# A four-layer graph network: more node-stage work on GpSimd, a bias by TensorE, and sums zeroed by ScalarE

## The reference, cut to what matters

```python
h = maximum(layernorm(x), 0); x = x + gat(h)      # layer 0, 8 heads of 16, self loops
h = maximum(layernorm(x), 0); x = x + gcn(h)      # layer 1
h = maximum(layernorm(x), 0); x = x + pna(h)      # layer 2
h = maximum(layernorm(x), 0); x = x + gatv2(h)    # layer 3
```

## Time and profile before

| | before |
|---|---|
| median of three runs | 4756.52 us (4754.43 to 4757.53) |
| profiled execution, its own time | 4756.6 us |
| span of that execution | 4754.8 us |
| mean granted TensorE clock | 0.729 |
| PE busy | 3336.3 us (70%) |
| PEld busy | 2878.0 us (61%) |
| DVE busy | 3192.4 us (67%) |
| ACT busy | 2417.6 us (51%) |
| POOL busy | 3323.1 us (70%) |

### The profile page before, as it was taken

One profiled execution on the slowest core, in us unless ns is written; L12 is line 12 of the kernel. 1 busy time (PEld: TensorE's weight loads), 2 busy tenths in 40 slices (PEclk: granted clock), 3 DMA queues, 4 the chain that ended last, 5 costly groups with the idle time before them and its releaser, 6 DMA issues. The chain is left out here.

```text
span 4754.8 us, 95466 instructions
## 1 busy us (share of the span) xinstructions
PE 3336.3 (70%) x21401; PEld 2878.0 (61%) x21402; DVE 3192.4 (67%) x8183; ACT 2417.6 (51%) x5426; POOL 3323.1 (70%) x3505
## 2 busy tenths in 40 slices
PE   3888888887533333334577777777696888888886
PEld 2666666666533333333476676767564777777775
DVE  5888888888533333334677777787656676666767
ACT  3666666665300000000577777777535666666664
POOL 4777777775677777776677777777524777777774
PEclk7555555555755566655799999899897888888887
DMA  7333333332122121111366666666422333333332
GB/s 131 88 84 86 86 84 86 86 86 54 49 52 53 53 53 53 53 53 44 120 184 184 185 185 185 181 186 183 145 63 50 76 79 80 80 80 80 79 78 72
DMA packets 367220, 462.19 MB, mean 97 GB/s; under 512 B 104067, under 2 KB 271235, under 8 KB 367104
## 3 DMA queue, kind: packets, MB, share of 16 engines
q0 software_dynamic: 107648, 226.35, 20.4%
q1 hardware_dynamic: 254176, 233.02, 16.3%
q10 hardware_dynamic: 5280, 1.58, 0.1%
HBM read 327.40 MB, written 134.06 MB: 97 GB/s over the span
## 5 line engine op out<-in xcount | busy, mean ns | idle before, releaser
L856 POOL DMA_INDIRECT e_G<-dr_tab,src_idx x832 | 810.3, 974 | 266.6 <-issue 253.2
L856 POOL DMA_INDIRECT m_G<-dr_tab,src_idx x832 | 798.2, 959 | 262.7 <-issue 246.4
L856 POOL DMA_INDIRECT v_G<-dr_tab,src_idx x832 | 791.5, 951 | 264.5 <-issue 248.3
L1749 POOL DMA_INDIRECT s_G<-dr_tab,chunk_src x784 | 740.0, 944 | 241.9 <-issue 238.6
L1837 PE MATMUL s_OUT<-s_G,s_S 128*128 x1664 | 380.2, 421 | 586.1 <-SPq L1781 578.4
L1837 PEld LDWEIGHTS s_OUT<-s_G,s_S 128*128 128x128 f32 x1664 | 354.7, 324 | 611.4 <-issue 611.4
L1793 DVE TENSOR_TENSOR ACC<-ACC,s_OUT 128x129 f32 x832 | 241.3, 290 | 604.5 <-PE s_OUT L1837 500.8
L1261 PE MATMUL e_OUT<-e_RH,e_S 128*128 128x144 f32 x1664 | 512.4, 476 | 2.4 <-DVE e_RH L1147 2.4
L2277 ACT COPY f_AT<-r_TP 128x512 f32<-128x512 f32 (+1 forms) x13 | 7.2, 555 | 973.6 <-PE r_TP L2299 973.6
L1994 DVE TENSOR_TENSOR ACC<-ACC,m_OUT 128x256 f32 x832 | 347.3, 417 | 222.3 <-PE m_OUT L2077 126.2
L1261 PEld LDWEIGHTS e_OUT<-e_RH,e_S 128*128 128x128 f32 x1664 | 405.3, 327 | 35.8 <-DVE e_RH L1147 18.4
(11 more groups left out here) (380 smaller groups left out, 8123.9 us busy)
## 6 DMA issues: line engine op xcount, KB each, us to landing
dr_ends<-m_XB SPq DMA_DIRECT2D x416, 256.0 KB, 3.2
e_LR<-dr_row_loc SPq DMA_DIRECT2D x104, 256.0 KB
m_MS<-dr_row_start SPq DMA_DIRECT2D x104, 256.0 KB
v_LR<-dr_row_loc SPq DMA_DIRECT2D x104, 256.0 KB
e_G<-dr_tab,src_idx POOLq DMA_INDIRECT x832
m_G<-dr_tab,src_idx POOLq DMA_INDIRECT x832
v_G<-dr_tab,src_idx POOLq DMA_INDIRECT x832
s_G<-dr_tab,chunk_src POOLq DMA_INDIRECT x784, 2.5
```

What stands on the lines that cost most here:

```text
L856: pool.indirect_dma_start(out=out, out_offset=None, in_=table, in_offset=bass.IndirectOffsetOnAxis(ap=g["src_idx"][:, step:step + 1], axis ...
L1749: pool.indirect_dma_start(out=G[:, c % (RING * GROUP), 0:D], out_offset=None, in_=table[:, :], in_offset=bass.IndirectOffsetOnAxis(ap=g["c ...
```

## The change

What it does, place by place:

- `gat_pass` and `moments_pass`: `ACC` is zeroed by an ACT instruction (a copy with scale 0 of a broadcast column) ahead of ACT's other work there, not by DVE's memset. `sum_pass` keeps its memset.
- `gat_pass`, behind the gathers: POOL computes the own loop's logit and 0.2 times it, in place in `XPA`; `gat_to_gcn` has two DVE instructions fewer.
- `gat_to_gcn`: POOL weighs the own rows (`by_head` with `es`), 13 pieces, and scales the table rows of the pieces 1, 3, 6, 8 and 11 (`on_pool`), behind its `add_rows` of the same piece. PE waits for both semaphores. SP waits, piece by piece, for the engine that scaled it.
- `pna_to_gatv2`: POOL normalises (`normalise_rows`: multiply and add with two scalars per row, without the rectifier), one piece behind its `row_root`; ACT rectifies when it copies the turned piece. PE adds the own rows' bias with one more product per tile (a row of ones by `b3`), and ACT copies them out negated, in place of DVE.
- The last block: DVE does pieces 0 to 6 as before. For pieces 7 to 12 ACT scales per tile, POOL adds the bias, ACT rectifies and POOL adds onto `X`. SP stores the pieces of both as they come.

The diff, cut to its core:

```diff
+        self.on_pool = [j for j in range(self.n) if j % 5 in (1, 3)]
...
+    def normalise_rows(self, pool, j):
+
+        pool.wait_ge(self.nmr_done, j + 1)
+        wait(pool, self.turned, j - self.R + 1)
+        for u in range(self.width(j)):
+            t = j * self.ch + u
+            ins = pool.tensor_scalar(self.H[:, j % self.R, u, :], self.g["X"][:, t, :], self.rstd[:, t:t + 1], self.nmr[:, t:t + 1],
+                                     ALU.mult, ALU.add)
+        ins.then_inc(self.h_done, 1)
...
+    def row_taken(self, j):
+
+        here = [i for i in range(j + 1) if (i in self.on_pool) == (j in self.on_pool)]
+        return (self.pool_taken if j in self.on_pool else self.taken), len(here)
...
-            out = self.HT[:, j % 2, 0:self.width(j), :]
-        self.nc.scalar.copy(out, self.TP[:, j % 2, 0:self.width(j) * P].rearrange("p (u n) -> p u n", n=P)).then_inc(self.ht_in, 1)
+            out, func = self.HT[:, j % 2, 0:self.width(j), :], ACT.Relu
+        self.nc.scalar.activation(out, self.TP[:, j % 2, 0:self.width(j) * P].rearrange("p (u n) -> p u n", n=P), func).then_inc(self.ht_in, 1)
...
+                pool.tensor_tensor(own_slope, own_slope, destination, ALU.add).then_inc(own_logits, 1)
+                pool.wait_ge(own_logits, 1)
+                pool.tensor_scalar(destination, own_slope, SLOPE, 0.0, ALU.mult, ALU.add).then_inc(own_logits, 1)
+                pool.wait_ge(own_logits, 2)
...
+                nc.scalar.activation(ACC[:].rearrange("p t c -> p (t c)"), g["ones"][:, 0:1].to_broadcast([P, TILES * AC]), ACT.Copy,
+                                     scale=0.0).then_inc(acc_done, 1)
...
-                V.memset(ACC[:], 0.0).then_inc(acc_done, 1)
...
+                nc.scalar.activation(ACC[:].rearrange("p t c -> p (t c)"), g["ones"][:, 0:1].to_broadcast([P, TILES * 2 * D]), ACT.Copy,
+                                     scale=0.0).then_inc(acc_done, 1)
...
-                V.memset(ACC[:], 0.0).then_inc(acc_done, 1)
...
+        def scale_rows(eng, j, done):
+            eng.tensor_tensor(T[:, st.tiles(j), :], st.H[:, j % st.R, 0:st.width(j), :],
+                              g["rs_out"][:, st.tiles(j)].unsqueeze(2).to_broadcast([P, st.width(j), D]), ALU.mult).then_inc(done, 1)
...
+                pool.wait_ge(chain, CHAIN)
+                for j in range(st.n):
+                    by_head(pool, XPA, es, j, own_scaled)
                 st.column_root(pool)
+                pool.wait_ge(rs_root, 1)
                 for j in range(st.n + 2):
                     if j < st.n:
                         st.row_root(pool, j)
                     if j >= 2:
                         st.add_rows(pool, j - 2)
+                        if j - 2 in st.on_pool:
+                            scale_rows(pool, j - 2, st.pool_taken)
...
-                    sp.wait_ge(st.taken, j + 1)
+                    sp.wait_ge(*st.row_taken(j))
...
+                    pe.wait_ge(rows_scaled, j + 1)
                     pe.wait_ge(own_scaled, j + 1)
...
-                c.then(V.tensor_tensor(es[:], XPA[:, :, D:D + HEADS], XPA[:, :, D + HEADS:], ALU.add))
-                c.then(V.tensor_scalar(mx[:], es[:], SLOPE, None, ALU.mult))
-                c.then(V.tensor_tensor(es[:], es[:], mx[:], ALU.max))
-                c.then(V.tensor_tensor(mx[:], r[:], es[:], ALU.max))
+                c.then(V.tensor_tensor(es, es, XPA[:, :, D + HEADS:], ALU.max))
...
-                        by_head(ACC, r, j, rows_scaled)
-                        by_head(XPA, es, j, own_scaled)
+                        by_head(V, ACC, r, j, rows_scaled)
...
-                    if i >= 0:
+                    if i >= 0 and i not in st.on_pool:
                         dve.wait_ge(st.h_done, i + 1)
-                        V.tensor_tensor(T[:, st.tiles(i), :], st.H[:, i % st.R, 0:st.width(i), :],
-                                        g["rs_out"][:, st.tiles(i)].unsqueeze(2).to_broadcast([P, st.width(i), D]),
-                                        ALU.mult).then_inc(st.taken, 1)
+                        scale_rows(V, i, st.taken)
...
-                for j in range(st.n):
-                    st.row_root(pool, j)
+                for j in range(st.n + 1):
+                    if j < st.n:
+                        st.row_root(pool, j)
+                    if j >= 1:
+                        st.normalise_rows(pool, j - 1)
...
-                for j in range(st.n + 3):
+                for j in range(st.n + 4):
                     if j < st.n:
                         st.apply(act, j)
-                    if 0 <= j - 2 < st.n:
-                        st.normalise(act, j - 2)
-                    if j >= 3:
+                    if 0 <= j - 3 < st.n:
                         st.turned_in(act, j - 3)
+                    i = j - 4
+                    if i >= 0:
+                        act.wait_ge(st.product, i + 1)
+                        nc.scalar.activation(XR[:, st.tiles(i), :], OP[:, 2 * (i % 2) + 1, 0:st.width(i) * D].rearrange("p (u d) -> p u d", d=D),
+                                             ACT.Copy, scale=-1.0).then_inc(xr_in, 1)
...
+                        wait(pe, xr_in, i - 1)
                         for u in range(st.width(i)):
                             nc.tensor.matmul(OP[:, 2 * (i % 2), u * (D + 1):(u + 1) * (D + 1)], st.HT[:, i % 2, u, :],
                                              g["W3"][:, 0:D + 1], start=True, stop=True)
-                            ins = nc.tensor.matmul(OP[:, 2 * (i % 2) + 1, u * D:(u + 1) * D], st.HT[:, i % 2, u, :],
-                                                   g["W3"][:, D + 1:2 * D + 1], start=True, stop=True)
+                            own = OP[:, 2 * (i % 2) + 1, u * D:(u + 1) * D]
+                            nc.tensor.matmul(own, g["ones"][0:1, :], g["b3"][0:1, D + 1:2 * D + 1], start=True, stop=False)
+                            ins = nc.tensor.matmul(own, st.HT[:, i % 2, u, :], g["W3"][:, D + 1:2 * D + 1], start=False, stop=True)
...
-                                        per_feature(g["b3"][:, 0:D + 1], w), ALU.add)
-                        V.scalar_tensor_tensor(XR[:, st.tiles(i), :], OP[:, 2 * (i % 2) + 1, 0:w * D].rearrange("p (u d) -> p u d", d=D), -1.0,
-                                               per_feature(g["b3"][:, D + 1:2 * D + 1], w), ALU.mult, ALU.subtract).then_inc(st.taken, 1)
+                                        per_feature(g["b3"][:, 0:D + 1], w), ALU.add).then_inc(st.taken, 1)
...
-                for j in range(NCH):
+                for j in range(HERE):
...
+            @block.scalar
+            def _(act):
+                def rectify(j):
+                    tl = slice(j * CH, min((j + 1) * CH, TILES))
+                    act.wait_ge(biased, j - HERE + 1)
+                    nc.scalar.activation(ACC[:, tl, 1:D + 1], ACC[:, tl, 1:D + 1], ACT.Relu).then_inc(rectified, 1)
+
+                act.wait_ge(denominators, 2)
+                for j in range(HERE, NCH):
+                    for t in range(j * CH, min((j + 1) * CH, TILES)):
+                        ins = nc.scalar.activation(ACC[:, t, 1:D + 1], ACC[:, t, 1:D + 1], ACT.Copy, scale=rd[:, t:t + 1])
+                    ins.then_inc(scaled, 1)
+                    if j > HERE:
+                        rectify(j - 1)
+                rectify(NCH - 1)
+
+            @block.gpsimd
+            def _(pool):
+                def add(j):
+                    tl = slice(j * CH, min((j + 1) * CH, TILES))
+                    pool.wait_ge(rectified, j - HERE + 1)
+                    pool.tensor_tensor(g["X"][:, tl, :], g["X"][:, tl, :], ACC[:, tl, 1:D + 1], ALU.add).then_inc(other_rows, 1)
+
+                for j in range(HERE, NCH):
+                    tl = slice(j * CH, min((j + 1) * CH, TILES))
+                    pool.wait_ge(scaled, j - HERE + 1)
+                    pool.tensor_tensor(ACC[:, tl, 1:D + 1], ACC[:, tl, 1:D + 1], per_feature(g["bias3"][:], tl.stop - tl.start), ALU.add).then_inc(biased, 1)
+                    if j > HERE:
+                        add(j - 1)
+                add(NCH - 1)
...
+                for j in range(HERE):
                     sp.wait_ge(out_rows, j + 1)
-                    sp.dma_start(rows[:, j * CH:(j + 1) * CH, :], g["X"][:, j * CH:(j + 1) * CH, :]).then_inc(stored, 16)
-                sp.wait_ge(out_rows, NCH)
+                    store(j)
+                    if 2 <= j < 2 + NCH - 1 - HERE:
+                        sp.wait_ge(other_rows, j - 1)
+                        store(HERE + j - 2)
```

More of the change, by code:

```diff
@@ L811, in normalise @@
             wait(act, self.xh_done, j - self.R + 1)
-        wait(act, self.turned if self.TP is not None else self.taken, j - self.R + 1)
+        if self.TP is not None:
+            wait(act, self.turned, j - self.R + 1)
+        elif j >= self.R:
+            act.wait_ge(*self.row_taken(j - self.R))
         for u in range(self.width(j)):
@@ L833, in turned_in @@
         act.wait_ge(self.turned, j + 1)
```

(59 more changed lines are left out.)

3 lines of the change are left out of this document (2 added, 1 removed).

## The result

The changed kernel took 4815.44 us (median of four runs, 4814.07 to 4820.07); the kernel before 4757.02 us beside it. The ratio is 1.0122 (95% interval 1.0108 to 1.0135): 1.2% slower, where no measurable change was forecast, and outside the range given. The profiled execution has a span of 4818.3 us, 63.5 more than before. It was the slowest of the four (4820.07 us); by the medians the loss is 58.4 us.

The account below looks back on a forecast made before the run. No engine was full; POOL's gather after gather was taken to bound the edge passes. The terms -6.7 - 12.9 - 0.4 + 2.0 + 9.6 + 4.1 gave -4.3, so 4756.6 became 4752.3 us, range 4738 to 4766.

Parts of the forecast that it names:

- Step 5: Second half of pna_to_gatv2: POOL's normalising and PE's bias products lengthen each two-piece turn, +9.6 us, bounds +5 and +20.
- c: Time of one POOL tensor_scalar when normalising in pna_to_gatv2: between 0.20 and 0.46 us, taken as 0.33.
- rival 2: pna_to_gatv2, second half: POOL's normalising is dear; at 0.78 us per instruction the whole takes 4763.1 us; chance 0.12.
- the prediction's ring: Second half of pna_to_gatv2: chain through the engines, turning once per two pieces, from 5.35 us to 6.55 us.
- Step 1: GAT pass: with ACT zeroing the sums, DVE's memset no longer holds POOL's gather, so the pass ends 6.7 us earlier.
- step 3: gat_to_gcn, chain and first half: two DVE instructions fewer and POOL weighing own rows, -0.4 us, bounds -1.0 and +8.
- step 2: Moments pass: with ACT zeroing, the first gather is no longer held by DVE's memset, -12.9 us.
- Rival 3: GAT and moments passes: the memset is not what held the gathers, so no gain there, 4771.9 us; chance 0.06.
- Steps 3, 4 and 6: gat_to_gcn first half -0.4 us, its second half +2.0, last stage +4.1, with POOL and DVE taking turns.

Follow-up runs that it names:

- e1: The changed kernel with the own rows' bias added by a product with all 128 rows in place of one; 4763.50 us, ratio 1.0009.
- e2: The kernel before with only the one-row bias product per tile in pna_to_gatv2 added, DVE only negating the own rows; 4823.53 us, ratio 1.0132.
- e9: The changed kernel with the bias product over 32 rows in place of one (own rows come out wrong); ratio 1.0092.
- e10: The changed kernel with the bias product over 64 rows in place of one (own rows come out wrong); ratio 1.0051.
- e7: The kernel before with only POOL normalising in pna_to_gatv2 and ACT rectifying in the copy, no bias product; ratio 1.0014.
- e5: The kernel before with each of DVE's two memsets split into an odd count and a single element; ratio 0.9988.
- e8: The changed kernel with pna_to_gatv2 as in the kernel before; ratio 0.9988.
- e3: The changed kernel with one one-row bias product per piece, 384 columns wide, in place of one per tile; 4778.20 us, ratio 1.0035.

## Why the prediction was wrong

**Step 5 failed, in its words "PE gets three bias products at 0.11 us: +0.33".** The price was taken from products of 128 rows at the upper clock, for one that uses one row among products that use 128. Even with 128 rows it was too low: each f32 product stands as two rows of 0.11, so 0.66 us a piece (e1: one every 0.22 us). With one row it brought two costs that the sum has no term for: the wait of 0.22 us before the loads on both sides of it, and a granted clock that stays at 0.50 while PE is fully busy. The bound of +20 for that part varied only POOL's c; it took PE's clock as given. (The low bound is off as well: by the prediction's own formula c = 0.20 with hidden products gives 8 x 0.48 = +3.8, not +5.) The slower side was priced in rival 2 by POOL's instruction, and the loss came from PE.

Both signs stood in the trace of before, outside the stage that was priced. In the GAT pass products of 1 and of 64 rows lie among those of 128: PE was busy 170 of 200 us there at a granted clock of 0.50, and the loads of one of its one-row products had 0.28 us of waits each in front of them (29.5 over 104). In the moments pass, whose steps have products of 128 rows only, PE was busy 367 of 500 us and the clock was at 0.92. The GAT pass in a stretch, one load of it by group, and the moments pass, in the kernel before:

```profile
300.00:500.00 200.00, 170.09 (x863) 134.19 (x863) 170.66 (x591) 137.44 (x320) 152.03 (x158) 0.50 0.36 85
L1241 PEld LDWEIGHTS e_ET<-eye,e_state_f 1*64 1x64 f32 x104 | 12.9, 124 | 29.5 <-issue 28.5 <-DVE e_ET L1121 1.0
2500.00:3000.00 500.00, 367.31 (x2795) 346.15 (x2794) 388.97 (x501) 386.36 (x799) 377.89 (x401) 0.92 0.61 184
```

The two passes differ in much else, so this is a sign and no proof; e1, e2, e9 and e10 are the proof.

The Trainium skill has a rule near the first of the two (TensorEngine Tiling (Array Packing), Key Properties): changing the tiling mode drains TensorE; the page's modes have tiles of 32, 64 or 128 rows. It does not say which mode a product of few rows takes. The traces agree so far as the waits stand at 1, 32 and 64 rows, and not at 128. The prediction did not weigh it.

**The rest of step 5 held.** With the measured c of 0.448 its formula gives 5.35 + 1.21 + 1.34 - 1.33 = 6.57 us per two pieces, 8 x 1.22 = +9.8; e7 measured +9.2. With bias products of 0.66 it is 9.8 + 8 x 0.66 = +15.1 (0.66 once per turn, as the prediction's ring counts its bias products); e1 measured +15.9. c itself lay at the top of the bounds (0.20 to 0.46), not at 0.33.

**Step 1 was mis-sized: 0 to 3.4 us in place of 6.7.** POOL did run gather after gather, and its last gather started 5.4 us earlier (1140.2 against 1145.6), counted from the pass's first gather 6.6 us, as predicted. But hardly anything was waiting for it. The waits of DVE in the kernel before say so:

```profile
DVE e_Z L1096 <- DMA e_G<-dr_tab,src_idx: 3.0, 3, 1.7
```

In the whole pass the gathers were late three times, for 3.0 us together, and faster gathers can bring about that and little more (the runs show 0 to 3.4, and e2, whose pass is unchanged, lies 0.6 off). POOL's idle 19.21 us at the pass's end, which the prediction used as cover in step 3, said the same. The last sums were added at 1164.49 in both kernels. In the moments pass PE did wait for gathers (196.5 us in 74 waits in the kernel before), and step 2 came in whole: -13.2 for -12.9.

**Rival 3 is refuted, by e5.** The Trainium skill's rule (SBUF — State Buffer, the practical consequences) names the even-count memset as an exception for the next chip only; the measurement decides: on this chip an even count of f32 holds POOL's gathers, an odd one does not.

**Steps 3, 4 and 6 had the mechanism and were near the size.** -0.3 for -0.4; +0.9 for +2.0 (e8: +0.6); +1.6 for +4.1. In the last stage, turns instruction for instruction would have ended DVE's work after 26.1 us. The changed kernel's trace has DVE's end and the last store as

```profile
4812.40 0.69 DVE L2723 SCALAR_TENSOR_TENSOR X<-ACC,X 128x512 f32<-128x512 f32 x1
4814.14 0.46 SPq L2770 DMA_DIRECT2D out_dram<-X  x1
```

so DVE, which began at 4791.13, ended 22.0 us later, exactly as long after its beginning as before with all 13 pieces: of POOL's 13.6 us it lost 9.5. The 1.6 us come from the end: before, the last store was that of a one-tile piece and was issued 0.03 us after DVE's last row; now it stands behind the store of a whole piece on SP, 1.05 us after that row, and the rest is its landing.

**Open.** The gatv2 pass, which the change doesn't touch, took 7.1 us more in the profiled execution after the change and 6.6 in e3, but 1.6 in e1 and 2.8 in e2. It goes neither with the clock at which the half ended nor with anything else that was varied. It shows as POOL's waits for ACT's `v_RH` ahead of a gather: 33.0 us in 51 waits after the change and 34.4 in e3, against 16.2 before, 18.5 in e1 and 22.1 in e2; why there are more of them stays open. Nor was it tried what makes the clock stay low at 32 rows and not at 64; the runs only show that it does.

## What to carry to other kernels

A product's price depends on its neighbours: before putting a one-row or 32-row product between 128-row products, write it with all rows (here the unit matrix by the bias on every partition), or leave the bias with the engine that had it. Look in the whole trace for products of that kind, not only in the stage that changes. An engine without waits is not yet the bound of a pass: ask who waits for its results and for how long, since that sum is about the most a faster one can bring. And before work moves to POOL to lie beside VectorE, look at VectorE's operands: with two in SBUF the two engines took turns here (four VectorE instructions of 1.14 us together took 4.83 beside POOL's adds), while beside ScalarE's scalings VectorE's instructions kept their 0.69 us.

## What was not expected of the hardware

- TensorE was busy 90.00 of 90.00 us and stayed at a granted clock of 0.50 with a one-row or 32-row product per tile; with a 64-row product in its place it was at 0.99, from 25 us after the half began.
- A memset of 12543 f32 elements and one of 12544 take the same 10.51 us, and only the even one holds GpSimd's gathers.
- POOL's multiply and add with two scalars per row took 0.448 us over 128x128, about as long as its add of two operands (0.456 at the least).
